# Six attention layers on one core: the output projection, the projection of k and the addition of rotated k take other places in their queues

## The reference

```python
qkv = x @ Wqkv                       # 16 heads of 64
q, k, v = (sh(q), sh(k), sh(v))
q = l2norm(q) * qs
k = l2norm(k) * ksc
q = q * cos * scale + rotate_half(q) * sin * scale
k = k * cos * inv + rotate_half(k) * sin * inv
...
sim = jnp.einsum('bhwie,bhwje->bhwij', bq, bk2) * QK_SCALE     # windows of 32 queries, 64 keys
sim = jnp.where(mask, -jnp.finfo(sim.dtype).max, sim)
attn = jax.nn.softmax(sim, -1)
out = jnp.einsum('bhwij,bhwje->bhwie', attn, bv2)
...
return out @ Wo                      # added to x
```

## Time and profile before

| | |
|---|---|
| median of three runs | 3972.0 us (3942.24 to 3986.53) |
| profiled execution: time, span | 3974.68 us, 3972.7 us |
| TensorE, VectorE, ScalarE, GpSimd busy | 79%, 73%, 53%, 30% of the span |
| TensorE's granted clock, mean | 0.911 |
| first addition of rotated k, end | 1834.22 us |

### The profile page before, as it was taken

How to read it: one execution, slowest core, us unless ns; L and a number is a source line. 1 busy time by engine, 2 the same in 40 slices (tenths; PEclk the granted TensorE clock), 3 DMA queues, 4 the chain that set the end, 5 groups by cost and what they waited for, 6 DMA issues and landing times. The chain is left out here.

```text
span 3972.7 us, 66964 instructions
## 1 busy us (share of the span) xinstructions
PE 3139.6 (79%) x25619; PEld 1696.4 (43%) x25853; DVE 2894.4 (73%) x4198; ACT 2103.0 (53%) x3147; POOL 1200.3 (30%) x628
## 2 busy tenths in 40 slices
PE   3899999995432888985888788788878878888887
PEld 1122222221221333323664566466546646664664
DVE  4788888884762788846776787688678768876875
ACT  2366666665220455564654565466556546654664
POOL 2000000000011000005563565356455535653561
PEclk7799999997765999997989898999999899999999
DMA  3200000000014000001101111001111011110100
GB/s 93 38 1 1 1 1 1 1 1 6 0 62 58 1 1 1 1 25 45 33 28 34 34 33 44 24 28 33 40 28 33 28 34 33 33 45 22 33 28 22
DMA packets 56646, 100.32 MB, mean 25 GB/s; under 512 B 19782, under 2 KB 38148, under 8 KB 54916
## 3 DMA queue, kind: packets, MB, share of 16 engines
q1 hardware_dynamic: 56324, 95.92, 9.2%
HBM read 37.95 MB, written 7.34 MB: 11 GB/s over the span
## 5 line engine op out<-in xcount | busy, mean ns | idle before, releaser
L456 DVE TENSOR_REDUCE a_part<-ps 128x1 f32<-128x512 f32 (+3 forms) x1664 | 1010.7, 656 | 336.0 <-PE ps L330 302.2
L440 ACT ACTIVATE a_Pb<-ps 128x1024 f32<-128x1024 f32 (+3 forms) x832 | 778.4, 974 | 633.3 <-PE ps L406 626.9
L330 PE MATMUL ps<-a_KS,a_QS 128*128 128x512 bf16 (+3 forms) x1592 | 567.0, 385 | 103.4 <-DMA a_QS<-pieces 45.4
L1021 PE MATMUL ps<-l_w_qkv,l_XS 128*128 128x512 f32 x1152 | 557.0, 618 | 60.1 <-DVE l_qn L1390 16.9
L961 POOL TENSOR_TENSOR l_sine<-l_qn,l_tab 128x512 f32<-128x512 f32 x192 | 342.5, 1784 | 501.9 <-DVE l_qn L1390 501.7
L406 PE MATMUL ps<-a_QS,a_KS 128*128 128x512 bf16 (+3 forms) x1598 | 466.6, 368 | 22.9 <-DMA a_QS<-a_mrow 9.2
L1035 PE MATMUL ps<-ident,l_hat 128*128 128x128 f32 x1536 | 236.1, 304 | 268.2 <-DVE l_hat L1406 249.0
L383 PE MATMUL ps<-a_Pb,V 128*32 128x512 f32 (+3 forms) x3328 | 422.8, 580 | 2.6 <-ACT a_Pb L440 0.9
L330 PEld LDWEIGHTS ps<-a_KS,a_QS 128*128 128x128 bf16 x1664 | 145.2, 98 | 650.6 <-DVE a_part L456 573.2
L985 POOL TENSOR_TENSOR l_weights<-l_weights,l_rcp 128x1024 f32<-128x1024 f32 x96 | 273.8, 2852 | 443.7 <-DVE l_rcp L1427 443.7
L1377 DVE TENSOR_REDUCE l_bounded<-l_square 128x8 f32<-128x512 f32 x384 | 261.3, 685 | 148.6 <-ACT l_square L1231 125.9
(11 more groups left out here) (185 smaller groups left out, 4541.5 us busy)
## 6 DMA issues: line engine op xcount, KB each, us to landing
l_V_earlier<-l_V SPq DMA_DIRECT2D x96, 384.0 KB, 3.5
l_V_earlier<-l_V SPq DMA_DIRECT2D x96, 128.0 KB, 3.4
l_w_qkv<-in_L_ffn_Wqkv_dram SPq DMA_DIRECT2D x6, 1536.0 KB, 8.1
pieces<-a_piece SPq DMA_DIRECT2D x12, 512.0 KB, 2.6
a_KS<-pieces SPq DMA_DIRECT2D x48, 128.0 KB
a_QS<-pieces SPq DMA_DIRECT2D x48, 128.0 KB
l_w_o<-in_L_ffn_Wo_dram SPq DMA_DIRECT2D x6, 512.0 KB, 4.0
a_cos<-in_c_cos_dram SPq DMA_DIRECT2D x2, 1024.0 KB, 5.0
```

Of the source, the lines that this page charges most:

```text
L330: mm = e.matmul(bank[:, 0:width], QS[:, c, head, qt * P:(qt + 1) * P], KS[:, head, b * CH:b * CH + width], start=not masked, stop=True, sk ...
L440: e.activation(Pb[:, n % 2, 2 * p:2 * p + 2, a:CH], ps[:, 2 * p:2 * p + 2, a:CH], ACT.Exp)\
L456: e.tensor_reduce(part[:, u % 2, h * TC + qt, b:b + 1], ps[:, 4 + n % 2, 0:width], AX.X, ALU.max)\
L1021: e.matmul(ps[:, (V_BANK[T] if i == 2 else 0) + b, :], XS[:, T * P:(T + 1) * P], w_qkv[:, at:at + CH], start=True, stop=True).then_inc(s.v ...
```

## The change

Only calls within the three `attend` functions change places; no instruction is added or taken away, and every semaphore wait stays as it was. The wait of each call goes with it.

```diff
--- before.py
+++ after.py
@@ -1121,16 +1121,16 @@
                             project(l, 1, 0, 1)
                         turn(l, T, 0)
                         turn(l, T, 1)
+                        if T >= 2:
+                            out_project(l, T - 2)
                         turn(l, T, 2)
                         turn(l, T, 3)
-                        if T >= 2:
-                            out_project(l, T - 2)
+                        if ahead:
+                            project(l, T + 1, 1, 0)
+                            project(l, T + 1, 1, 1)
                         if T:
                             turn_weights(l, T - 1, 0)
                             turn_weights(l, T - 1, 1)
-                        if ahead:
-                            project(l, T + 1, 1, 0)
-                            project(l, T + 1, 1, 1)
                         scores(l, T, 0)
                         scores(l, T, 1)
                         if T:
@@ -1301,13 +1301,15 @@
                             inverse_norms(l, 1, 0)
                         for r in range(4):
                             store_qk(l, T, r)
-                        if T:
-                            place_low(l, T - 1, 0)
-                            place_low(l, T - 1, 1)
                         if ahead:
                             squares(l, T + 1, 1, 0)
                             squares(l, T + 1, 1, 1)
+                        if T:
+                            place_low(l, T - 1, 0)
+                        if ahead:
                             inverse_norms(l, T + 1, 1)
+                        if T:
+                            place_low(l, T - 1, 1)
                         if T:
                             store_o(l, T - 1, 0)
                             store_o(l, T - 1, 1)
@@ -1467,21 +1469,22 @@
                             e.wait_ge(s.added, START + l * NT + NT - 2)
                             for c in range(NC - 1):
                                 shift(c, s.xs)
+                        if ahead:
+                            sum_squares(l, T + 1, 1)
                         if T:
                             place_high(l, T - 1, 0)
+                        if ahead:
+                            normalise(l, T + 1, 1)
+                        if T:
                             place_high(l, T - 1, 1)
-                        if ahead:
-                            sum_squares(l, T + 1, 1)
-                            normalise(l, T + 1, 1)
                         maxima(l, T)
                         subtract(l, T)
                         if T + 2 < NT:
                             sum_squares(l, T + 2, 0)
                         if ahead:
                             cosines(l, T + 1, 1)
+                            add_rotated(l, T + 1)
                         sums(l, T)
-                        if ahead:
-                            add_rotated(l, T + 1)
                         if T + 2 < NT:
                             normalise(l, T + 2, 0)
                             cosines(l, T + 2, 0)
```

## The result

The changed kernel took 3758.96 us (median of four runs, 3743.41 to 3766.23) against 3960.3 us for the kernel before, measured beside it (median of four; the 3972.0 given above is the median of three of these). The ratio is 0.948, with a 95% interval of 0.941 to 0.955. Forecast were 3727 us and a range of 3685 to 3820. The profiled execution took 3765.1 us with a span of 3762.0, which is 210.7 us less span than before.

A forecast was written before the change was run, and what follows sets the result against it. Bound: a path from hat through TensorE's projection of k, squares, norms and VectorE, plus low clock. 72 turns at 15.9 us save 212, other intervals 36, together 248: 3974.7 - 248 = 3727 us, range 3685 to 3820.

The forecast's parts named there:

- The ring: Path of one tile's turn: addition of rotated k (hat), TensorE to k's projection, squares, norms, VectorE to next hat; 17.48 us.
- The clock: TensorE's clock falls after its 2.94 us wait for the hat; matmuls between transposes of q and k keep it at 1.00.
- like turns: The 72 turns from hat 2 to hat 14, twelve per layer: 18.84 us each before, 15.9 forecast, 212 us saved.
- Rivals A: TensorE's clock still falls in half of the turns: mean turn 16.75 us, time 3788 us; chance 0.10.
- E: Low clock spreads over weight turns, scores and values: turn 20.4 us, time 4051 us, slower; chance 0.03.
- The walk: Step-by-step timing of the new turn through VectorE and TensorE, from hat to hat: 15.85 us at full clock.
- the second half of the values: On TensorE, held to 9.0 us after the hat by VectorE's second copy, takes about 1.0, ends at 9.95.
- rival C: VectorE's second copy is late, delaying values and squares by 0.7 us: turn 16.6 us, time 3777 us; chance 0.07.
- The hat edit: Hat ahead of VectorE's sums and reciprocal moves 1.46 us to the front; meeting GpSimd's weights gives no own gain or loss.
- The split copies: First copy (0.7 us) fills VectorE's 0.83 us wait for inverse norms; without any gain from this the turn is 16.6 us.
- rival B: GpSimd's sine of q precedes VectorE's cosines, which wait 1.26 us more: time 3818 us; chance 0.07.
- The 18 other intervals: Intervals between hats 0 and 15 outside the 72 turns, 332.88 us before: lose 28 to 44 us, 36 taken.

The follow-up runs named there:

- out_only: The kernel before with only the output projection moved between the turns of q and of k: 3810.60 us, ratio 0.964.
- all_but_hat: The changed kernel with the addition of rotated k put back behind sums and reciprocal: 3722.38 us, ratio 0.944.
- all_but_out: The changed kernel with the output projection put back behind the turns of k: 3782.70 us, ratio 0.955.
- the filled kernel: The kernel before with eight unread matmuls added between the turns of q and k, nothing moved: 3865.07 us, ratio 0.976.
- The repeated kernel: The changed kernel run once more, with nothing altered: 3749.45 us, ratio 0.946.
- fill_transpose: The kernel before with sixteen unread transposes added between the turns of q and k, nothing moved: 3887.51 us, ratio 0.982.
- hat_only: The kernel before with only the addition of rotated k moved ahead of the softmax sums: 3829.35 us, ratio 0.972.

## Why the prediction was right, and where its sizes were off

*What bounds the kernel.* Right. The ring from hat through the projection of k, squares and norms back to VectorE was the path. Beside the output projection the projection of k (with the split copies) shortens it, from 16.58 in out_only to 15.96 in all_but_hat, and the output projection takes another 0.22 (all_but_out); alone, the projection of k with the split does not (17.74 for 17.48).

*The clock.* Right, and by experiment: a filled wait keeps 1.00 on an unchanged path (in 71 of 72 like turns with matmuls, in all with transposes). Of the 191.5 us that the like turns lost, 100 are clock (the filled kernel has them all) and 72 x (17.45 - 16.18) = 91 are path. Rivals A and E did not come: no like turn of the changed kernel has a low stretch. Where the prediction took over, from the Trainium skill, "TensorE: Matmul & The Clock Gate", Part 4: PE-mode transpose, that transposes do not count as activity, the measurement decides otherwise: sixteen transposes held 1.00 as well as matmuls.

*The turn.* 15.85 was worked out, 16.20 measured. The walk held up to the subtraction: cosines done at 4.48 for 4.55, squares summed at 6.08 for 6.21, maxima at 8.96 for 8.85, subtraction done at 11.44 for 11.32. The term that was mis-sized is the second half of the values, taken as 1.0 us. It started at 9.07 and took 1.15, to 10.22 instead of 9.95; the squares of q were then 0.27 late, and VectorE waited 0.60 instead of 0.44. Another 0.09 is the start of the hat behind the cosines (0.14 instead of 0.05). The copy itself was on time (8.92 for 8.93), so rival C's condition, a late copy, did not come; what stands behind it was late by less than half of C's 0.7. In the sum it is 1165.3 - 1144.8 = 20.5 us.

*The hat edit.* Here a step failed. The prediction weighed the cosines of q beside GpSimd's weights and held that this "gives no gain or loss of its own". With the two TensorE edits in place it is a loss: without the hat edit the turn is 15.96, with it 16.20, and the cosines are 1.61 and 1.86. The sum was not wrong by it, since the walk had the cosines done at 4.55 (measured 4.48); but it was never set against the turn without the edit.

*The split copies.* Here another step failed. The prediction took the split as a gain, since the first copy fills the 0.83 us wait for the inverse norms, and put a turn without that gain at 16.6. It did not weigh both copies directly behind the squares' sums, which fill the same wait: that turn is 15.45, so against this order the split costs 0.75. No run puts both copies back ahead of the squares' sums in the changed kernel, so the 0.7 of the 16.6 is not shown. The measured time fell near the forecast all the same, because the walk followed the queues as they stand and had the cost of both edits in it; what it had wrong is which of them earned anything.

*GpSimd beside VectorE.* Right as read: VectorE came next when the weights finished, rival B did not come.

*The rest.* The 18 other intervals lost 332.9 - 299.8 = 33 us for 36. Behind the layers next to nothing changed (74.99 for 75.04 behind layer 2), as taken, and for the reason weighed: the residual comes 1.32 earlier and the first shift copy takes 1.63 instead of 0.42. Ahead of the layers, where nothing was edited, the profiled execution was 12.5 us later (first hat at 1846.74 instead of 1834.22). With the 20.5, 3 and 1 of the tails that is the whole of 248 - 211. The repeated kernel started at 1830.61, so these 12.5 are what executions differ by.

## What to carry to other kernels

A wait of TensorE on the path costs twice where the clock falls behind it, and other work of its own put into the wait is a cure; look for the granted clock of single turns, since a mean of 0.91 hides turns of 1.00 and 0.83. Be careful with holding back a copy that another engine waits for: one held back to fill a wait of 0.8 us made values, projection and squares queue up behind it, which cost 0.75. Test the edits of a bundle singly and left out singly, since one that gains alone (the hat, 2.8%) may cost in the bundle, and one that gains nothing at full clock alone (the projection of k) may gain there.

## What the runs showed of the hardware

Fp32 transposes kept the granted clock at 1.00 just as matmuls did: with 1.91 us of them in the wait of 2.94 (fill_transpose) all like turns had 1.00, and 17.48 us (17.21 in the last layer).

A wait of 1.61 us in one piece (all_but_out) let the clock fall in none of the 72 like turns, nor did one of 1.61 with 0.52 behind turns of k and output projection (hat_only). Waits of 1.15 and 0.67 us with 1.09 us of transposes between (out_only) did in three turns of twelve, while the 1.15 alone (all_but_hat) did not. The runs do not settle which property of that stretch decides.

VectorE's cosines (two SBUF inputs) took 1.22 us alone, and 1.61 (before) or 1.86 (changed) when they began while GpSimd was at its weights. In both cases they ended 1.08 us after the weights did, wherever they had begun, which fits one waiting for the other to end. GpSimd's weights took 1.90 us when they came first and 2.96 when VectorE's hat did.
